# Routing of a mixture of experts: one-hots in batches of four, with broadcast operands and two factors on the tile's one-hot

## What is computed

```python
raw_gate = softmax(einsum('btd,de->bte', x, gate))
_, topk_idx = top_k(raw_gate, 3)
gate_topk = mask * raw_gate                       # mask: the three experts of a token
gate_topk = gate_topk / max(sum(abs(gate_topk)), EPS)
hidden = relu(einsum('btd,edh->bteh', x, W1) + b1)
expert_out = einsum('bteh,ehd->bted', hidden, W2) + b2
return einsum('bte,bted->btd', gate_topk, expert_out)
```

## Time and profile before

| | us |
|---|---|
| median of three runs (2014.85 to 2018.07) | 2014.93 |
| the profiled execution, its own time | 2014.51 |
| its span, first to last instruction | 2012.8 |
| attention, setup included | to about 1358 |
| routing | about 1358 to 1508.4 |
| of that, the loop over the pairs | 1452.0 to 1504.2 |
| experts | 1509.4 to about 1936 |
| combine | about 1939 to the end |

### The profile page before, as it was taken

The page is one execution under the profiler, slowest core; times in us unless marked ns, Lnnn a source line. Parts: engine busy times, 40 slices in busy tenths (PEclk is TensorE's granted clock), DMA queues, the critical chain, the costliest instruction groups (busy, mean ns, idle before and its releaser), DMA issues. The chain is left out here.

```text
span 2012.8 us, 36193 instructions
## 1 busy us (share of the span) xinstructions
PE 1789.6 (89%) x10192; PEld 1321.7 (66%) x10193; DVE 1404.9 (70%) x2857; ACT 765.1 (38%) x1691; POOL 1181.8 (59%) x1086
## 2 busy tenths in 40 slices
PE   4589999999999999999999999974589999999940
PEld 4356667666666766766676676642248999999940
DVE  3368888887887887787887888755794454544448
ACT  3134444443443444444444444435351222222225
POOL 2256776676676666766766776643224555555544
PEclk9589999999999999999999999996659999999975
DMA  9776466555555655755664564409402222222255
GB/s 318 238 207 160 147 177 199 147 167 171 160 164 174 188 151 155 206 140 169 191 165 138 169 175 139 126 11 357 156 1 64 70 71 70 70 71 70 70 181 182
DMA packets 164538, 301.21 MB, mean 150 GB/s; under 512 B 18768, under 2 KB 57360, under 8 KB 163360
## 3 DMA queue, kind: packets, MB, share of 16 engines
q1 hardware_dynamic: 152608, 269.79, 44.7%
q0 software_dynamic: 10752, 29.37, 4.7%
q10 hardware_dynamic: 1024, 0.26, 0.1%
HBM read 192.15 MB, written 106.95 MB: 149 GB/s over the span
## 5 line engine op out<-in xcount | busy, mean ns | idle before, releaser
L687 ACT ACTIVATE prob<-b_ps 128x512 f32<-128x512 f32 (+3 forms) x768 | 357.3, 490 | 417.0 <-PE b_ps L531 319.4
L454 POOL TENSOR_TENSOR acc<-acc,prob 128x1024 f32<-128x1024 f32 (+1 forms) x192 | 351.1, 1829 | 22.4 <-issue 18.9
L756 DVE TENSOR_REDUCE max_b<-a_ps 128x1 f32<-128x512 f32 (+3 forms) x512 | 284.2, 571 | 80.9 <-PE a_ps L519 32.6
L530 PE MATMUL b_ps<-q,k 128*128 128x512 f32 (+3 forms) x768 | 312.0, 411 | 4.5 <-DMA q<-mrow 3.5
L427 POOL TENSOR_TENSOR roped<-rot 128x512 f32<-128x512 f32 x128 | 174.7, 1365 | 219.8 <-DVE rot L769 219.2
L519 PE MATMUL a_ps<-k,q 128*128 128x512 f32 (+3 forms) x768 | 274.0, 387 | 30.7 <-DVE max_b L756 20.0
L604 PE MATMUL y_ps<-prob,v_sb 128*64 128x512 f32 (+3 forms) x1536 | 273.4, 491 | 0.0
L531 PE MATMUL b_ps<-q,k 65*128 65x512 f32 (+3 forms) x768 | 265.8, 350 | 0.0
L1411 DVE TENSOR_SCALAR hT<-h_ps,b1T 128x128 f32<-128x128 f32 x448 | 126.2, 345 | 190.2 <-PE h_ps L1330 175.3
L795 DVE RECIPROCAL inv<-inv 128x128 f32<-128x128 f32 x256 | 231.9, 928 | 7.7 <-ACT inv L719 7.1
L432 POOL TENSOR_TENSOR lo<-roped,hi 128x512 fp32r<-128x512 f32 x128 | 178.1, 1391 | 85.6 <-ACT hi L700 85.6
(11 more groups left out here) (249 smaller groups left out, 2713.4 us busy)
## 6 DMA issues: line engine op xcount, KB each, us to landing
q<-scratch_hilo SPq DMA_DIRECT2D x192, 256.0 KB, 4.5
k<-scratch_hilo SPq DMA_DIRECT2D x192, 256.0 KB, 5.2
scratch_hilo<-hi SPq DMA_DIRECT2D x64, 512.0 KB, 3.9
scratch_hilo<-lo SPq DMA_DIRECT2D x64, 512.0 KB, 4.7
w_sb<-scratch_wsplit SPq DMA_DIRECT2D x32, 512.0 KB, 3.5
w<-in_L_ffn_W_dram SPq DMA_DIRECT2D x32, 512.0 KB, 10.2
got<-scratch_ys SPq DMA_DIRECT2D x32, 384.0 KB, 6.1
wv_sb<-scratch_wsplit SPq DMA_DIRECT2D x16, 512.0 KB, 6.5
```

The source lines that it names most:

```text
L454: nc.gpsimd.tensor_tensor(sums, old, probs(q), ALU.add).then_inc(m["sum_p"], 1)
L530: nc.tensor.matmul(out, k1[s][:, h, js], q1[s][:, h, qs], start=True, stop=False, skip_group_check=True)
L687: nc.scalar.activation(probs(q)[:, h, :], b_ps[:, h, 0:w], ACT.Exp).then_inc(exp_done[h], 1)
L756: nc.vector.tensor_reduce(out, a_ps[:, h, 0:w], AX_X, ALU.max, negate=True).then_inc(a_max[h], 1)
```

## The change

- The loop runs over 24 batches of four pairs. `HOT` is 4, and each one-hot has two buffers of four pairs. A batch is four neighbouring token tiles of one k, since `row_of` and `tile_of` (now bf16) are read as k x token tile.
- DVE makes `tile_hot` of a batch in one instruction and `row_hot` in another, each a comparison of two tensors with broadcast operands. `tile_hot` has no factor any more.
- The factors go onto `tile_hot`: `coded` holds for each pair two blocks of 112 columns, `tile_hot` times the token's number (by ACT, in every third batch by DVE), and `tile_hot` times the batch's number plus one (always by ACT). `row_hot_k` is gone.
- PE has one product per pair, `row_hot` x both blocks, 224 columns wide. Pair b of a batch adds into its own quarter of `tr_ps`, four sums in all; which quarter holds a slot tells b. `inv_ps` is gone.
- The bias product 10 + a stands on PE behind the products of batch a; on ACT its eviction stands behind the factors of batch a.
- Behind the loop, DVE adds up the four quarters, finds b by a comparison, and needs no reciprocal.
- Places in `ys` are (k x 32 + token tile) x 128 + number, and the combine stage reads them so.

```diff
-        HOT = 8
+        HOT = 4
+        BATCHES = TOPK * TILES // HOT
...
+        def part_by_dve(a):
+            return a % 3 == 0
...
-            for i in range(last + 1):
-                pe.wait_ge(m["r_oh"], i + 1)
-                nc.tensor.matmul(inv_ps[:, 0:SLOT_TILES], row_hot[:, i % HOT, :], tile_hot[:, i % HOT, :],
-                                 start=(i == 0), stop=(i == last), skip_group_check=True)
-                pe.wait_ge(m["r_oh_k"], i + 1)
-                nc.tensor.matmul(tr_ps[:, 0, 0:SLOT_TILES], row_hot_k[:, i % HOT, :],
-                                 tile_hot[:, i % HOT, :], start=(i == 0), stop=(i == last),
-                                 skip_group_check=True).then_inc(m["r_inv"], 1)
-                if i % 4 == 0 and EARLY_BIASES + i // 4 < TILES:
-                    weighted_biases(EARLY_BIASES + i // 4)
+            for a in range(BATCHES):
+                pe.wait_ge(m["r_row"], a + 1)
+                pe.wait_ge(m["r_part"], a + 1)
+                pe.wait_ge(m["r_code"], a + 1)
+                for b in range(HOT):
+                    c0 = b % 2 * 2 * SLOT_TILES
+                    ins = nc.tensor.matmul(tr_ps[:, b // 2, c0:c0 + 2 * SLOT_TILES], row_hot[:, a % 2, b, :],
+                                           coded[:, a % 2, b].rearrange("p v c -> p (v c)"),
+                                           start=(a == 0 and b % 2 == 0), stop=(a == BATCHES - 1),
+                                           skip_group_check=True)
+                ins.then_inc(m["r_inv"], 1)
+                if EARLY_BIASES + a < TILES:
+                    weighted_biases(EARLY_BIASES + a)
...
-            for i in range(TOPK * TILES):
-                t, k = i // TOPK, i % TOPK
-                act.wait_ge(m["r_oh_a"], i + 1)
-                if i >= HOT:
-                    act.wait_ge(m["r_inv"], i - HOT + 1)
-                nc.scalar.activation(row_hot_k[:, i % HOT, :], row_hot[:, i % HOT, :], ACT.Copy,
-                                     scale=float(PLACES * t + k + 1)).then_inc(m["r_oh_k"], 1)
-                if i % 4 == 3 and EARLY_BIASES + i // 4 < TILES:
-                    take_biases(EARLY_BIASES + i // 4)
+            for a in range(BATCHES):
+                act.wait_ge(m["r_tile"], a + 1)
+                if a >= 2:
+                    act.wait_ge(m["r_inv"], a - 1)
+                nc.scalar.activation(coded[:, a % 2, :, 1, :], tile_hot[:, a % 2], ACT.Copy, scale=float(a + 1))\
+                    .then_inc(m["r_code"], 1)
+                if not part_by_dve(a):
+                    act.wait_ge(m["r_part"], a)
+                    nc.scalar.activation(coded[:, a % 2, :, 0, :], tile_hot[:, a % 2], ACT.Identity, scale=part[:, 0:1])\
+                        .then_inc(m["r_part"], 1)
+                if EARLY_BIASES + a < TILES:
+                    take_biases(EARLY_BIASES + a)
...
-            for i in range(TOPK * TILES):
-                t, k = i // TOPK, i % TOPK
-                if i >= HOT:
-                    dve.wait_ge(m["r_inv"], i - HOT + 1)
-                V.tensor_scalar(row_hot[:, i % HOT, :], ioq[:], row_of[:, k, t:t + 1], None, ALU.is_equal)\
-                    .then_inc(m["r_oh_a"], 1)
-                V.tensor_scalar(tile_hot[:, i % HOT, :], ioq[:, 0:SLOT_TILES], tile_of[:, k, t:t + 1],
-                                part[:, 0:1], ALU.is_equal, ALU.mult).then_inc(m["r_oh"], 1)
+            for a in range(BATCHES):
+                some = slice(HOT * a, HOT * (a + 1))
+                if a >= 2:
+                    dve.wait_ge(m["r_inv"], a - 1)
+                    dve.wait_ge(m["r_code"], a - 1)
+                V.tensor_tensor(tile_hot[:, a % 2], bt(ioq[:, 0:SLOT_TILES], HOT), bc(tile_of[:, some], SLOT_TILES),
+                                ALU.is_equal).then_inc(m["r_tile"], 1)
+                V.tensor_tensor(row_hot[:, a % 2], bt(ioq[:], HOT), bc(row_of[:, some], P), ALU.is_equal)\
+                    .then_inc(m["r_row"], 1)
+                if part_by_dve(a):
+                    dve.wait_ge(m["r_tile"], a + 1)
+                    dve.wait_ge(m["r_part"], a)
+                    V.tensor_scalar(coded[:, a % 2, :, 0, :], tile_hot[:, a % 2], part[:, 0:1], None, ALU.mult)\
+                        .then_inc(m["r_part"], 1)
...
-        ys = dram["ys"][0:NTOK * PLACES, :].rearrange("(t k p) d -> t p k d", k=PLACES, p=P)
+        ys = dram["ys"][0:NTOK * TOPK, :].rearrange("(k t p) d -> t p k d", k=TOPK, p=P)
```

More of the change, by code:

```diff
@@ L852, in routing_phase @@
         iot = sb("iot", [P, SLOT_TILES], F32)
[L853 to L860, removed]
+        oh_mask = sb("oh_mask", [P, TOPK + 1, TILES, E_], F32)
+        oh, mask = oh_mask[:, 0:TOPK], oh_mask[:, TOPK]
+        hot = oh_mask[:].rearrange("p k t e -> p (k t e)").bitcast(BF16)
+        ends = np.cumsum([0, 2 * HOT * P, 2 * HOT * SLOT_TILES, 4 * HOT * SLOT_TILES])
+        row_hot = hot[:, ends[0]:ends[1]].rearrange("p (s i c) -> p s i c", s=2, i=HOT)
+        tile_hot = hot[:, ends[1]:ends[2]].rearrange("p (s i c) -> p s i c", s=2, i=HOT)
+        coded = hot[:, ends[2]:ends[3]].rearrange("p (s i v c) -> p s i v c", s=2, i=HOT, v=2)
         maskb = sb("gmaskb", [P, TILES, E_], BF16)
         tot = sb("tot", [P, E_, TILES], F32)
-        back = tot[:].rearrange("p e t -> p (e t)")[:, 0:2 * SLOT_TILES].rearrange("p (i c) -> p i c", i=2)
+        back = tot[:].rearrange("p e t -> p (e t)")[:, 0:4 * SLOT_TILES].rearrange("p (i c) -> p i c", i=4)
         inc = sb("inc", [P, E_, TILES], F32)
@@ L870, in routing_phase @@
         sloti = sb("sloti", [P, 3, TOPK, TILES], I32)
-        row_of = sb("row_of", [P, TOPK, TILES], F32)
-        tile_of = sb("tile_of", [P, TOPK, TILES], F32)
+        row_of = sb("row_of", [P, TOPK * TILES], BF16)
+        tile_of = sb("tile_of", [P, TOPK * TILES], BF16)
         part = sb("part", [P, 1], F32)
@@ L931, in _ @@
             pool.memset(ident[:], 0.0).then_inc(m["r_const"], 1)
-            for t, pattern, base, mult in ((ioq, [[1, P]], 0, 0), (unused, [[P, SLOT_TILES]], PLACES * NTOK + P, 1),
+            for t, pattern, base, mult in ((ioq, [[1, P]], 0, 0), (unused, [[P, SLOT_TILES]], PLACES * NTOK + HOT * P, 1),
                                            (part, [[0, 1]], 1, 1)):
@@ L1209, in _ @@
             link(V.tensor_scalar(sloti[:, 2], sloti[:, 0], 7, None, ALU.logical_shift_right))
[L1210 to L1211 removed]
+            V.tensor_copy(row_of[:], sloti[:, 1].rearrange("p k t -> p (k t)"))
+            V.tensor_copy(tile_of[:], sloti[:, 2].rearrange("p k t -> p (k t)")).then_inc(m["r_slots"], 1)
             dve.wait_ge(m["r_slots"], 1)
[L1213 to L1224 removed]
+            for a in range(BATCHES):
[12 more added lines that the diff above has]
+                        .then_inc(m["r_part"], 1)
+                if a < E_:
+                    if a == 0:
@@ L1225, in _ @@
                         ins = V.tensor_scalar(ef[:], iot[0:1, :], cnt[0:1, 3, 0:1], None, ALU.is_ge)
                     else:
-                        dve.wait_ge(m["r_ef"], e)
-                        ins = V.scalar_tensor_tensor(out=ef[:], in0=iot[0:1, :], scalar=cnt[0:1, 3, e:e + 1], in1=ef[:],
+                        dve.wait_ge(m["r_ef"], a)
+                        ins = V.scalar_tensor_tensor(out=ef[:], in0=iot[0:1, :], scalar=cnt[0:1, 3, a:a + 1], in1=ef[:],
                                                      op0=ALU.is_ge, op1=ALU.add)
@@ L1233, in _ @@
             link(V.tensor_copy(etile[:], ef[:]))
[L1235 to L1248, removed]
+            dve.wait_ge(m["r_inv"], BATCHES)
+            found = tr_ps[:, :, 0:4 * SLOT_TILES]
@@ new lines, in _ @@
+            spare = inc[:].rearrange("p e t -> p (e t)")
+            both, place, more = spare[:, 0:4 * SLOT_TILES].rearrange("p (u c) -> p u c", u=2), back[:, 0, :], back[:, 1, :]
+            V.tensor_reduce(both, found.rearrange("p u (v c) -> p u c v", v=2), AX_X, ALU.add)
+            for u in range(2):
+                codes = found[:, u].rearrange("p (v s c) -> p v s c", v=2, s=2)[:, :, 1, :]
+                ins = V.scalar_tensor_tensor(out=back[:, 2 * u:2 * u + 2, :], in0=codes, scalar=0.5,
+                                             in1=bc(ioq[:, 2 * u:2 * u + 2], SLOT_TILES), op0=ALU.is_gt, op1=ALU.mult)
@@ new lines, in _ @@
+            link(ins)
+            sums = slots[:].rearrange("p t e -> p (t e)")
+            total, which = sums[:, 0:2 * SLOT_TILES], sums[:, 2 * SLOT_TILES:3 * SLOT_TILES]
+            V.tensor_tensor(total, both[:, 0, :], both[:, 1, :], ALU.add)
+            link(V.tensor_reduce(which, back.rearrange("p i c -> p c i"), AX_X, ALU.add))
+            row = spare[:, 0:SLOT_TILES]
+            V.tensor_scalar(row, total[:, 0:SLOT_TILES], -1.0, 0.0, ALU.add, ALU.max)
+            link(V.scalar_tensor_tensor(out=place, in0=total[:, SLOT_TILES:], scalar=float(HOT), in1=which, op0=ALU.mult,
+                                        op1=ALU.add))
@@ L1249, in _ @@
```

(12 more changed lines are left out.)

4 lines of the change are left out of this document (1 added, 3 removed).

## The result

| | before | after |
|---|---|---|
| median, us (4 runs each) | 2015.44 (2014.85 to 2018.07) | 2044.86 (2043.45 to 2047.29) |
| profiled execution, its own time | 2014.51 | 2043.45 |
| span | 2012.8 | 2041.7 |
| loop, first one-hot to DVE's first sum | 1452.0 to 1504.2: 52.2 | 1454.1 to 1533.2: 79.1 |
| chain behind the loop | 4.2 | 5.0 |

The changed kernel is 1.45% slower: ratio 1.0145, 95% interval 1.0127 to 1.0162. Forecast were 2042, a range of 2032 to 2050, and a loop of 78.8 us.

A forecast was written before the change was run, and what follows sets the result against it. The prediction took DVE to bound the loop before, and PE and ACT taking turns after. From 2014.5 us, +26.6 for the loop and +0.4 for the chain gave 2041.5, at the median 2041.9; forecast 2042, range 2032 to 2050.

The forecast's parts named there:

- The bound of before: Loop before the change: DVE sets the length, 37.0 + 3.8 + 11 = 51.8 us, with PE close behind.
- The turn: Changed loop: PE's and ACT's shares no longer overlap; rounds of 3.59 or 3.05 us, loop 78.8 against 52.2, +26.6 us.
- DVE's share: DVE's work in the loop: 1.15 us per batch for both one-hots, 1.84 in all, under the round.
- the double rate: DVE's one-hots: lower bound of 0.6 us for the two if bf16 doubled the speed; not expected with broadcast operands.
- What goes with it: Loop: POOL's 0.5 us delays and `ef` steps covered by DVE's waits; fewer products and scalings already in the sum.
- The chain behind the loop: DVE's operations after the loop: 4.6 us against 4.2, so +0.4 us.
- The result's places: Expert rows' new order in writing and combine-stage reading: taken as 0, upward bound some 9 us.
- The total: Whole kernel: 2014.5 + 26.6 + 0.4 = 2041.5, so 2041.9 us at the median.
- DVE's pace: Rival for the loop: without turns it runs at DVE's 1.84 us per batch, total 2008.8 us; chance 0.03.
- the rival of a rising clock: Rival for the loop: PE's clock rises to 2.4 GHz, rounds of 2.60 and 2.06 us, total 2019.7; chance 0.07.

The follow-up runs named there:

- e3: The kernel before without the 22 bias products, evictions and additions in its loop; loop 41.1 us, total 2005.61 us, ratio 0.9943 to the kernel before.
- e1: The changed kernel with ACT's eviction of each bias product one step later; loop 48.3 us, total 2010.68 us, ratio 0.9981 to the kernel before.
- e6: The changed kernel with evictions later and bias products issued in pairs behind every second batch; loop 46.7 us, total 2010.17 us, ratio 0.9972 to the kernel before.
- e7: The changed kernel with three idle bf16 products behind each batch on PE; loop 81.6 us, total 2045.62 us, ratio 1.0145 to the kernel before.

## Why the prediction was right

**The bound of before.** Right. e3 confirms the sum by which it was read: without the bias work the loop is 41.1 us, which is 96 x 0.385 + 16 x 0.24 = 40.8.

**The turn.** Right, in kind and in size. Forecast were rounds of 3.59 and 3.05 us; the timeline has 3.59 and 3.09. Its terms against the trace: three further products and the step to the bias product, 0.56 + 0.30, measured 0.84 (1459.26 to 1460.10); bias product to eviction 1.25 and eviction to code factor 0.28, as read before; code factor to token factor 0.46, measured 0.47; token factor 0.66, measured 0.657; its end to the next product 0.07, measured 0.09. In the short round this last step is 0.15 (1465.79 to 1465.94), which is where 3.09 in place of 3.05 comes from. The code factor by itself was forecast at 0.577 and took 0.568:

```profile
L1228 DVE TENSOR_TENSOR oh_mask<-ioq,row_of 128x512 bf16<-128x512 bf16 x24 | 16.4, 684 | 0.0
...
L1100 ACT ACTIVATE oh_mask<-oh_mask 128x448 bf16<-128x448 bf16 x24 | 13.6, 568 | 2.1 <-DVE oh_mask L1226 2.1
...
L1104 ACT ACTIVATE oh_mask<-oh_mask,part 128x448 bf16<-128x448 bf16 x16 | 10.5, 657 | 0.0
```

**DVE's share.** Right: 0.54 and 0.60 us from start to start, from fp32 comparisons with broadcast operands. That the operands are bf16 brings nothing, since 512 columns take 0.684 mean (L1228 above) against 0.69 in the earlier trace rows. So the double rate, which the prediction left as a lower bound, is not there. The Trainium skill ("VectorE: DVE Perf Modes", "What auto-detection actually checks") grants it only if every tensor is 16-bit with step ±1, which the broadcast operand is not; the trace agrees with 0.684.

**What goes with it.** Right: the 22 additions and the `ef` steps lie in DVE's waits, and the first batch starts on PE 1.58 us after the first one-hot (forecast 1.5).

**The chain behind the loop.** The sign was right, the size off: 5.0 us, so +0.8 in place of +0.4. The term that was too small is the sum of four places per slot. It was priced as an ordinary reduction of 448 elements, and reads its operand across four rows of `back`:

```profile
1533.24 1.09 DVE L1251 TENSOR_REDUCE inc<-tr_ps 128x448 f32<-128x896 f32 x1 [3.10 <-PE tr_ps L1042]
...
1535.27 0.90 DVE L1260 TENSOR_REDUCE slots<-tot 128x112 f32<-128x448 f32 x1
```

0.90 where the prices of the earlier trace rows give 0.6. That the order of reading is the reason is likely and not shown; no run reads the same elements contiguously.

**The result's places.** Right at 0 or a little better: the combine stage lasts 73.1 us (from 1968.65) against 73.9 before, and DVE waits 7.3 us for the first tiles against 8.56, in one execution of each:

```profile
1968.65 11.63 SPq L1480 DMA_DIRECT2D got<-scratch_ys  x14
...
1976.12 2.47 DVE L1559 SCALAR_TENSOR_TENSOR x<-got,wts,x 128x256 f32<-128x256 f32 x6 [7.34 <-DMA got<-scratch_ys]
```

**The total.** Of the span's 28.9 us more, 26.9 are the loop, 0.8 the chain, 2.1 lie ahead of the loop, and the rest gives 0.9 back. Of the 2.1, 1.9 are there when the attention stage makes its last store (1356.60 and 1358.54), in code that is the same in both. They are scatter of that stage, which the prediction did not price: over all runs the kernel before ranges from 2004.7 to 2025.2 us.

**The rivals.** DVE's pace did not decide, since the round never came near 1.84 us. The prediction also had this rival's floor wrong. It said that without turns the loop would run at DVE's 1.84 us, but four products and a bias product occupy PE for 0.84 + 1.15 = 1.99 us. e1, with the turns gone, runs at 2.0 us and 48.3 us in all, not at 45.7; only with the bias products in pairs as well (e6) does the loop come to 46.7. The forecast did not use that floor. The clock stayed at 0.50 also with PE busy for 76.40 of 81.60 us (e7), which speaks further against the rival of a rising clock.

## What to carry to other kernels

When two engines serve each other twice in one loop (here PE waits for ACT's factors, and ACT for PE's bias product), look at which instruction stands directly in front of the one that the other engine needs next. If it waits for that engine's newest work, the two take turns and the round is the sum of their shares, however much slack each has; one step of delay of the eviction took back 30.8 us. The mirror image, the bias product ahead of the batch's own products on PE, was not run. A rewrite that makes instructions fewer and wider can also remove the small ones that had filled such a wait, as ACT's three scalings had here, so that the order of what remains has to be set anew.

## What the runs showed of the hardware that I had not expected

- The granted clock stayed at 0.50 for the whole loop in every kernel, with PE busy for 46.96 of 79.1 us, 50.97 of 52.2, or 76.40 of 81.60 with fillers, bf16 or fp32. In the gate stage it was 1.00 with PE busy 17.3 of 20 us. Busy time does not tell which level holds; the cause stays open.
- A POOL addition can take over three times its usual time while DVE is busy without a break. In e6 DVE goes from one wide instruction to the next, and one addition, begun at 1471.98, takes 3.54 us; that DVE holds it up is my reading, and no run tests it. Six instructions of DVE pass, from 1472.08 on, before one at 1474.85 is lengthened in its turn, to 0.80; the median of the additions is 0.97. The next eviction waited 0.77 us for it:

```profile
1471.98 3.54 POOL L955 TENSOR_TENSOR x<-xtt,x 128x256 f32<-128x256 f32 x1
...
1475.61 0.38 ACT L1092 ACTIVATE xtt<-bb_ps 128x256 f32<-128x256 f32 x1 [0.77 <-POOL x L955]
```

  It happens at two places in e6's loop (the other begins at 1460.01), where POOL's busy time is 26.28 us against 15.88 in the changed kernel, for the same 22 additions. The prediction had only the reverse, POOL's addition that delays DVE by 0.5 us.
- Pairs of fp32 products on different 32-row groups ran at once inside the loop (e6): 1.2 us for both, as long as one alone in e1 (1.22). Such a pair ahead of the loop had shown it before, so this one was expected.
